# A decoder stack on one core: the last feed-forward's gelus move behind the last exponential, and identity products stand where TensorE waited

## The reference, cut to what matters

```python
def _decoder_block(x, enc, ...):
    h = _layernorm(x, ln1_w, ln1_b)                    # self-attention, 16 heads of 16
    ...
    h = _layernorm(x, ln2_w, ln2_b)                    # cross-attention over enc
    q, k, v = ...
    attn = jax.nn.softmax(jnp.where(enc_mask, neg, einsum(q, k) * scale), axis=-1)
    x = x + (attn @ v) @ out_w + out_b
    h = _layernorm(x, ln3_w, ln3_b)                    # feed-forward, 1024 wide
    h = jax.nn.gelu(h @ mlp1_w + mlp1_b, approximate=False)
    return x + h @ mlp2_w + mlp2_b
```

## Time and profile before

| | |
|---|---|
| runs | 1550.68, 1553.16, 1554.07 us; median 1553.16 |
| profiled execution | 1551.07 us, span 1548.9 us |
| PE busy | 1499.6 us (97%) |
| ACT, DVE, POOL busy | 1011.8, 916.0, 841.8 us |
| mean granted TensorE clock | 0.993 |

### The profile page before, as it was taken

One profiled execution on the slowest core, in us unless ns is written; L12 is line 12 of the kernel. 1 busy time (PEld: TensorE's weight loads), 2 busy tenths in 40 slices (PEclk: granted clock), 3 DMA queues, 4 the chain that ended last, 5 costly groups with the idle time before them and its releaser, 6 DMA issues.

```text
span 1548.9 us, 37237 instructions
## 1 busy us (share of the span) xinstructions
PE 1499.6 (97%) x13750; PEld 1304.2 (84%) x13750; DVE 916.0 (59%) x2474; ACT 1011.8 (65%) x2934; POOL 841.8 (54%) x1400
## 2 busy tenths in 40 slices
PE   7999999999999999999999999999999998899998
PEld 7888888888889888878888889878888887778878
DVE  7566544455567655654554566654555568867774
ACT  6667667666661656767666672566666678678871
POOL 3665357676553544546676645346676646744431
PEclk9999999999999999999999999999999999999998
DMA  6223110001111200211000121111000121011000
GB/s 205 76 86 123 62 32 19 19 19 45 44 48 35 81 1 15 69 49 36 20 19 19 45 65 38 55 43 36 19 19 19 43 66 34 18 34 34 19 1 25
DMA packets 41617, 67.24 MB, mean 43 GB/s; under 512 B 8352, under 2 KB 16352, under 8 KB 41440
## 3 DMA queue, kind: packets, MB, share of 16 engines
q1 hardware_dynamic: 40848, 64.71, 13.1%
q10 hardware_dynamic: 592, 0.17, 0.1%
HBM read 59.33 MB, written 5.54 MB: 42 GB/s over the span
## 4 chain that ended last, share of the span: by engine, by line
PE 85%; DVE 6%; ACT 4%; issue 3%; POOL 2%; DMA 0%; SPq 0%; DVEq 0%; ACTq 0%; POOLq 0%
PE pG L1345 49%; PE pO L1345 13%; PE pG L1541 12%; PE pS L1345 10%; ACT P L1725 1%; DVE KF L1865 1%; DVE nmax L1847 1%; DVE W L1795 1%; PE pG L1598 1%; ACT QF_hi L1669 0%; DVE bn L1777 0%; DVE full L1930 0%; POOL P L1992 0%; DVE x L1910 0%; DMA whole_f<-wts 0%
## 5 line engine op out<-in xcount | busy, mean ns | idle before, releaser
L1992 POOL TENSOR_SCALAR P<-P,rinv 112x375 f32<-112x375 f32 (+1 forms) x640 | 325.8, 522 | 244.2 <-DVE rinv L1871 243.7
L1725 ACT ACTIVATE P<-pS,nmax 112x375 f32<-112x375 f32 (+1 forms) x640 | 307.9, 496 | 102.6 <-DVE nmax L1847 102.6
L1345 PE MATMUL pG<-hT_hi,W 128*128 128x224 f32 (+2 forms) x1312 | 298.1, 306 | 9.0 <-DVE W L1795 3.5
L1738 ACT ACTIVATE PT<-pG 125x336 f32<-125x336 f32 (+1 forms) x448 | 198.5, 469 | 79.4 <-PE pG L1541 78.5
L1345 PEld LDWEIGHTS pG<-hT_hi,W 128*128 128x128 f32 x1312 | 222.4, 192 | 22.7 <-issue 4.1
L1541 PE MATMUL pG<-ident,P 112*125 112x112 f32 (+1 forms) x1472 | 225.4, 278 | 8.8 <-ACT PT L1738 2.8
L1847 DVE TENSOR_REDUCE nmax<-pS 112x1 f32<-112x375 f32 (+1 forms) x448 | 227.4, 549 | 6.9 <-PE pS L1345 5.3
L1345 PE MATMUL pG<-src,W 128*128 128x376 f32 (+1 forms) x956 | 220.8, 354 | 0.3 <-ACT whole_f L1673 0.2
L1541 PEld LDWEIGHTS pG<-ident,P 112*125 112x125 f32 (+1 forms) x1472 | 185.8, 176 | 41.3 <-ACT PT L1738 5.3
L1345 PE MATMUL pG<-hT_lo,W 128*128 128x224 f32 (+2 forms) x656 | 194.9, 297 | 0.0
L1345 PEld LDWEIGHTS pG<-src,W 128*128 128x128 f32 (+1 forms) x956 | 158.9, 189 | 27.7 <-issue 25.2
(11 more groups left out here) (142 smaller groups left out, 2893.2 us busy)
## 6 DMA issues: line engine op xcount, KB each, us to landing
wraw<-wts SPq DMA_DIRECT2D x110, 256.0 KB, 2.5
src<-ctx_split SPq DMA_DIRECT2D x64, 282.0 KB, 3.1
ctx_split<-hid_lo_t SPq DMA_DIRECT2D x8, 564.0 KB, 3.6
whole_f<-wts SPq DMA_DIRECT2D x14, 256.0 KB, 5.9
V<-ctxT SPq DMA_DIRECT2D x8, 376.0 KB, 4.0
src_half<-ctx_split SPq DMA_DIRECT2D x21, 94.0 KB, 3.2
bo_b<-bo SPq DMA_DIRECT2D x10, 128.0 KB, 3.3
wraw<-wts SPq DMA_DIRECT2D x8, 64.0 KB
```

What stands on the lines that cost most here:

```text
L1345: return nc.tensor.matmul(o, l, r, start=first, stop=last)
L1725: ins = act.activation(o, pS[U % 4][0:T, i * n:(i + 1) * n], ACT.Exp, bias=nmax[:, r, i:i + 1], accum_out=rsum[:, r, i:i + 1])
L1738: act.activation(o[0:sh.krows, 0:n], g[0:sh.krows, 0:n], ACT.Copy).then_inc(pt_ready, 1)
L1992: ins = pool.tensor_scalar(o, o, rinv[:, r, i:i + 1], st.nscale, ALU.mult, ALU.mult)
```

## The change

`GELUS[6]` goes from groups of six and two column tiles to groups of five and three. `GELU_AFTER[6]` goes from ((2, 1), (3, 2)) to ((3, 2), (3, 3)): the first gelu is put behind the exponentials of set 3 and the copies of set 2, the second behind the exponentials of set 3 and the copies of set 3. TensorE's list gets four blocks of identity transposes (a new task kind `warm`), and the block ahead of the first `qk` has 34 in place of 12. A `qk` task waits for the query weights first and for the key weights only ahead of its seventh matmul.

```diff
-GELUS = {1: ((0, 1, 2), (3, 4, 5), (6, 7)), 3: ((0, 1, 2), (3, 4, 5), (6, 7)), 6: ((0, 1, 2, 3, 4, 5), (6, 7))}
-GELU_AFTER = {1: ((1, 0), (2, 1), (3, 3)), 3: ((1, 0), (2, 1), (3, 3)), 6: ((2, 1), (3, 2))}
+GELUS = {1: ((0, 1, 2), (3, 4, 5), (6, 7)), 3: ((0, 1, 2), (3, 4, 5), (6, 7)), 6: ((0, 1, 2, 3, 4), (5, 6, 7))}
+GELU_AFTER = {1: ((1, 0), (2, 1), (3, 3)), 3: ((1, 0), (2, 1), (3, 3)), 6: ((3, 2), (3, 3))}
...
-    return order
+    return [f for e in order for f in ([e, Ev("warm", 6, B - 1, 0, WARM[e])] if e in WARM else [e])]
+
+WARM = {Ev("trans", 6, B - 1, 10): 8, Ev("trans", 6, B - 1, 11): 4, Ev("av", 6, B - 1, 3): 5, Ev("ta", 6, B - 1): 9}
...
+        elif e.kind == "warm":
+            needs.append(("dve", Ev("scores", 6, B - 1, H - 4)))
...
                 needed = chunks_of(e) if e.kind in PIECES else []
+                if e.kind == "qk":
+                    needed = needed[:len(needed) // 2]
                 if needed:
                     weight_split(pe, max(w_no[ch] for ch in needed) - 1)
...
-            def turn_nothing(n):
+            def turn_nothing(bank, n):
                 for _ in range(n):
-                    nc.tensor.transpose(pO[:, 0:128], ident[:, :], ident[:, :])
+                    nc.tensor.transpose(bank[:, 0:128], ident[:, :], ident[:, :])
...
                 if e == Ev("qk", 0, 0, 0):
-                    turn_nothing(12)
+                    turn_nothing(pO, 34)
...
                     for n, (slot, col, ks) in enumerate((st.q, st.k)[:len(e.kind)]):
                         passes = []
+                        if n:
+                            weight_split(pe, max(w_no[ch] for ch in chunks_of(e)) - 1)
...
+                elif e.kind == "warm":
+                    wait(pe, maxed, unit_no(6, B - 1, H - 4) + 1)
+                    turn_nothing(pS[unit_no(6, B - 1, H - 4) % 4], e.m)
```

More of the change, by code:

```diff
@@ L469, in tail @@
     if s == 6:
-        out = [held[0]] + scored + [Ev("lnt", ff.ln, NTILE - 2), held[1], Ev("ta", s, B - 1), Ev("tb", s, B - 1), Ev("ff2", s, 0), Ev("wo", s, NTILE - 1), Ev("ff2", s, 1), Ev("lnt", ff.ln, NTILE - 1), Ev("ff2", s, 2)] + [Ev("ffg", s, 1, t) for t in range(8)] + [Ev("ff2", s, 3), Ev("ff2", s, 4), Ev("ff2", s, 5), Ev("ff2", s, 6)]
+        gates = [Ev("ffg", s, 1, t) for t in range(8)]
+        out = [held[0]] + scored + [Ev("lnt", ff.ln, NTILE - 2), held[1], Ev("ta", s, B - 1), Ev("tb", s, B - 1), Ev("ff2", s, 0), Ev("wo", s, NTILE - 1), Ev("ff2", s, 1), Ev("lnt", ff.ln, NTILE - 1), Ev("ff2", s, 2)] + gates
+        out += [Ev("ff2", s, j) for j in range(3, NTILE)]
         return out
@@ L528, in duration @@
             return .75 if st.small else 2.83
-        return dict(ta=.48, tb=.27, q=.68, qk=1.36, k=.69 if joined(e.s, e.b) else .86, kk=.5 if e.m else .26, vp=.94, lnt=.23, ffg=1.06 if e.b else 1.4, ffa=1.06 if e.b else 1.4, ff2=2.83)[k]
+        return dict(warm=.11 * e.m, ta=.48, tb=.27, q=.68, qk=1.36, k=.69 if joined(e.s, e.b) else .86, kk=.5 if e.m else .26, vp=.94, lnt=.23, ffg=1.06 if e.b else 1.4, ffa=1.06 if e.b else 1.4, ff2=2.83)[k]
     if engine == "act":
@@ L1392, in _ @@
             pe.wait_ge(const_ready, 1)
-            def turn_nothing(n):
+            def turn_nothing(bank, n):
                 for _ in range(n):
-                    nc.tensor.transpose(pO[:, 0:128], ident[:, :], ident[:, :])
-            turn_nothing(18)
+                    nc.tensor.transpose(bank[:, 0:128], ident[:, :], ident[:, :])
+            turn_nothing(pO, 18)
             for e in order["pe"]:
```

## The result

| | before | after |
|---|---|---|
| median of 10 runs | 1553.09 us (1550.09 to 1554.07) | 1556.34 us (1556.08 to 1557.78) |
| profiled execution, span | 1548.9 us | 1554.2 us |
| mean granted clock | 0.993 | 0.995 |

The ratio is 1.0030 (95%: 1.0021 to 1.0039): the kernel became slower by about 4.7 us (3.3 to 6.1). The two medians lie 3.3 us apart, at the lower end of that, and the two profiled executions 5.3. The forecast was 1556.4.

The account below looks back on a forecast made before the run. TensorE's chain was taken as the bound (PE busy 97%), so only its waits and half-clock stretches count. Start -1.6 and end +5.8 gave +4.2 on 1552.24, so 1556.4 us; range 1551.3 to 1559.3.

Parts of the forecast that it names:

- Start: First 28 us: no clock fall at 12.75, DVE limits the gain; 1.6 us gained, bounds 0.67 and 2.26.
- the query half: First qk at the start: six matmuls run before the key weights are ready, gaining 0.67 us.
- Steps 1 to 4: Last attention: identities delay the fourth turn 0.9 us; gelu and table loads on ACT keep PE idle from 1506.05 to 1509.6.
- Step 5: DVE after the first gelu: splits of tiles 3 and 4 at 2.5 each, pO copy 1514.1, ta 2.6 us later.
- Steps 6 and 7: From ta to ff2 0: DVE's last two splits at 1.9 each put ff2 0 at 1520.35, 5.8 us later.
- Clock at the end: First 3.5 us of ff2 at half clock before and after alike, so no change of that term (1.7 us in both).
- The identities hold the clock at the end: Rival: clock at 2.4 GHz when ff2 0 starts, sum +0.8 us, 1553.0; chance 0.17.
- Nothing held at the start: Rival: clock falls near 12.75 us as before, start gives 0.67 only, 1557.4; chance 0.09.
- Hidden after all: Rival: DVE and POOL split side by side at 1.44, ff2 0 at 1517.9, total 1552 to 1553.5; chance 0.10.
- the bounds of 5.1 and 7.0: Delay of ff2 0 in us with DVE's last two splits both at 1.44 (5.1) or both at 2.50 (7.0).
- the prediction's 0.9 us: Before ff2 0: POOL's two splits end by 1519.4, hidden behind DVE's last split ending at 1520.3.
- The lower end of the range, 1551.3: Whole kernel: fastest time allowed, named for a start gain of 2.26 us with the clock held.

Follow-up runs that it names:

- e8: Kernel before with only the 34 identities at the start added; first projection still waits for both weight halves, end as before: 1550.30 us, ratio 0.9992 to before.
- e1: Only the change's start (34 identities, query half first), with the end of the kernel before and no blocks: 1549.97 us, ratio 0.9992 to before.
- e4: Changed kernel without early_exp behind the last feed-forward's first gelu, so two table loads fewer: 1555.80 us, ratio 1.0024 to before.
- e6: e1 with the gelus at the new place but still in groups of six and two, no identity blocks at the end: 1554.83 us, ratio 1.0021 to before.
- e7: e1 plus the change's four identity blocks at the end, gelus grouped and placed as before: 1548.18 us, ratio 0.9976 to before.
- e3: Changed kernel without its four identity blocks at the end (new start, gelus 5+3 at the new place): 1555.25 us, ratio 1.0025 to before.

## Why the prediction was right, step by step

The median fell on the forecast (1556.34 against 1556.4). By ratio the kernel lost 4.7 us where 4.2 were forecast. The mechanism held, but the hit to 0.1 us is luck. The forecast set out from 1552.24, where the ten runs of before have 1553.09. And its terms missed in opposite directions: in the profiled pair the start kept 0.53 us of 1.6, the end cost 5.28 for 5.8, and 0.55 us behind `ff2` 0 had been put at nothing, together 5.3 for 4.2.

*Start.* The clock did not fall at 12.75, DVE set the pace as forecast (its idle time went from 2.26 to 0.72 us of the 18.13), and by the turn at 36.04 (37.80 before) 1.8 us were gained where 1.6 were taken. The named source of 0.67 us, the query half, was not real (e8). What the prediction did not have: the time won is partly lost again. In the profiled execution the clock fell behind the wait that ends at 36.04 (0.72 in 35.00:41.00), which it had not done there in before (1.00). Of the 1.76 us, 1.10 were left at the wait that ends at 1299.18 (1300.28 before), and 0.51 at the one that ends at 1321.78 (1322.29), though the clock was at 1.00 between these two in both; what took that part was not traced. At the third turn it was 0.53. The fall at 36 us doesn't belong to the kernel: e1 and e8, with the same block of 34, show 1.00 there. Over many runs e1 and e8 keep about 1.2 us.

*Steps 1 to 4.* The eight identities delayed the fourth turn by 0.89 (1501.80 to 1502.68). TensorE's wait was forecast to end at 1509.6 on the axis of before; it ended at 1509.19, that is 1509.72 on that axis. The interpolated gelus took 2.34 and 1.48. These steps held; only the copies behind the wait and the second gelu ended 0.3 us earlier than forecast.

*Step 5.* The copy of pO was put at 1514.1; it came at 1511.75 (1512.28 on the axis of before). The size was off: the splits of tiles 3 and 4 took 1.45 and 2.50 us, 3.8 together and not 5.0, and `lnt`'s scaling was not late. The reading behind it was wrong: the prediction took 2.50 as the price beside a split of POOL's and 1.44 as the other one, but POOL was splitting beside both in before too (1511.86 to 1514.37, beside the one at 1511.81), and the first of the three splits of before took 2.14. `ta` then hung not on DVE but on the five identities ahead of it, which ran at half clock (5 x 0.21 = 1.1 us from 1511.59). So `ta` came 11.33 us behind the third turn, and not 12.24.

*Steps 6 and 7.* The two last splits took 2.0 each where 1.9 were taken; from the division's end to `ff2` 0 it was 4.8 us for 4.4. Together 5.28 us for 5.8, within the bounds of 5.1 and 7.0 (with both splits at 1.44 the prediction's own terms give 4.9, not 5.1). That the chain through DVE sets `ff2` 0, and not the table loads as such, is what e4 shows. The forecast path had its last step right, but POOL's queue lay closer behind it than the prediction's 0.9 us, and took its place in e6.

*Clock at the end.* Forecast the same in both. It was close (rest 34.9 against 34.4), though for another reason than thought: the blocks did raise the clock, and the 4.27 us wait undid it.

*The rivals.* "The identities hold the clock at the end" fell for this kernel at the point it named: the row from `ff2` 0 on shows 0.50. Its reasoning was sound where the wait is absent (e7: 1.00). "Nothing held at the start" fell: the row 12.75:16.05 shows 1.00 after 34 identities. So the trace doesn't agree with the rule of the Trainium skill (TensorE: Matmul & The Clock Gate, Part 4: PE-mode transpose) that the full clock does not engage for transposes. "Hidden after all" had `ta` right (1513.2, measured 1513.24 on that axis), nearer than the forecast itself, though with 1.44 us for each split of tiles 3 and 4; it missed by 1.9 us at `ff2` 0 (1517.9 against 1519.80), for the two splits behind the division. The lower end of the range, 1551.3, doesn't come out of the terms named for it; they give 1552.6, or 1551.6 with the `ff2` 0 of "hidden after all". The gelu at 1504.95 begins 0.01 us behind its table load. The drain of 1.38 us per switch that the Trainium skill states (ScalarE: Activation LUTs, What ACT_TABLE_LOAD costs) is not seen here either.

What the change is made of, by ratios in turn: start -1.2 us (e1), blocks -2.5 us (e7 against e1), gelus +8.4 us (after against e7). The last is 5.1 us for the gelus' new place and sizes (e3 against e1), the 2.5 us that the blocks no longer give, and 0.8 that they cost. The profiled executions of after and e7 say the same: `ff2` 0 comes 6.53 us later and 2.0 us more lie behind it. Each of these steps is uncertain by 1.5 to 2 us.

Left open: what makes one of DVE's splits take 1.45 us and the next 2.50, with POOL splitting beside both, and how far they would shrink without POOL's, was not measured; and why the clock falls at one wait of 1 to 2 us and not at the next is not settled.

## What to carry to other kernels

A long instruction on a side engine belongs where the main engine has work of its own; behind the last exponential ACT's copies were the next step of the chain, and everything that follows from the gelu's result queued up in DVE behind it. Fillers that keep TensorE's clock are worth it where they lie directly in a wait that is there anyway; in this case they served the work behind them only where no wait as long as the 4.27 us followed first. When runs of one kernel scatter more than the change under test moves them, look at the granted clock behind the main engine's waits of 1 to 2 us.

## What the runs showed of the hardware

Identity transposes can bring the granted clock up: at the start, where TensorE had done nothing before, 18 of them took 0.206 us each and, behind four more transposes, the next twelve 0.112. At the end of the kernel after, they and the work around them brought it from 0.50 to 0.99 at 1513.70. The mean granted clock of an execution can order the times of one kernel: e7's ten runs took 1548.9 to 1549.9 us at 0.996, 1547.5 at 0.998, 1546.6 and 1547.1 at 0.999, and 1545.3 at 1.000. It doesn't in every kernel: two runs of the kernel after took 1556.34 and 1556.31 us at 0.995 and 0.993. And the length of a wait alone doesn't tell whether the clock falls behind it: the wait at 36 us is 2.04 us long in before, 2.05 in after and 2.08 in e1 and e8, and only in after the clock fell behind it.
